# Row sums and shift rows by VectorE's block transposes and transfers instead of by TensorE

## The reference, cut to what matters

```
h = layernorm(x) * (1 + ca) + sa
xq, xk, xv = h @ wq.T, h @ wk.T, h @ wv.T         # 16 heads of 64, 2048 positions each
scores = softmax(xq @ xk.T * 64 ** -0.5)          # per head: 2048 x 2048, fp32
out = scores @ xv
x = x + ga * (out @ wo.T)
```

## Time and profile before

| | |
|---|---|
| median of 3 runs | 1318.63 us (1318.17 to 1810.67) |
| profiled execution, its own time | 1317.36 us |
| its span, first to last instruction | 1315.6 us |
| TensorE busy | 1297.5 us (99%) |
| POOL busy | 1176.0 us (89%) |
| VectorE busy | 911.3 us (69%) |
| ScalarE busy | 888.3 us (68%) |

### The profile page before, as it was taken

One profiled execution on the slowest core, in us unless ns is written; L12 is line 12 of the kernel. 1 busy time (PEld: TensorE's weight loads), 2 busy tenths in 40 slices (PEclk: granted clock), 3 DMA queues, 4 the chain that ended last, 5 costly groups with the idle time before them and its releaser, 6 DMA issues. The chain is left out here.

```text
span 1315.6 us, 22284 instructions
## 1 busy us (share of the span) xinstructions
PE 1297.5 (99%) x8792; PEld 705.3 (54%) x8792; DVE 911.3 (69%) x1036; ACT 888.3 (68%) x1096; POOL 1176.0 (89%) x538
## 2 busy tenths in 40 slices
PE   7999999999999999999999999999999999999998
PEld 5545545454555545454555555454545545454787
DVE  6767667676767677677767676776767676859575
ACT  6666767676766766666766666676767667775474
POOL 2499999999999999999999999999999999999644
PEclk9999999999999999999999999999999999999999
DMA  8010202020110202020100202020200102001323
GB/s 210 11 39 1 49 1 49 1 49 1 27 24 1 49 1 49 1 49 1 38 13 1 49 1 49 2 49 0 49 1 10 40 1 49 1 1 30 101 73 89
DMA packets 31962, 41.55 MB, mean 32 GB/s; under 512 B 4298, under 2 KB 15186, under 8 KB 31858
## 3 DMA queue, kind: packets, MB, share of 16 engines
q1 hardware_dynamic: 31714, 40.13, 12.5%
q10 hardware_dynamic: 144, 0.00, 0.0%
HBM read 13.70 MB, written 1.11 MB: 11 GB/s over the span
## 5 line engine op out<-in xcount | busy, mean ns | idle before, releaser
L918 ACT ACTIVATE probs<-ps 128x1024 f32<-128x1024 f32 x512 | 498.7, 1032 | 78.7 <-PE ps L1348 75.9
L1079 DVE TENSOR_REDUCE peak_parts<-ps 128x2 f32<-128x1024 f32 x297 | 362.2, 1223 | 236.8 <-PE ps L1289 235.1
L1366 PE MATMUL ps<-probs,v_sb 128*64 128x512 f32 x2048 | 522.8, 606 | 0.0
L1009 POOL TENSOR_TENSOR acc<-acc,probs 128x1024 f32<-128x1024 f32 x192 | 457.7, 2384 | 31.2 <-ACT probs L918 29.6
L1009 POOL TENSOR_TENSOR acc_odd<-acc_odd,probs 128x1024 f32<-128x1024 f32 x192 | 459.5, 2393 | 0.0
L860 ACT COPY peak_copy<-ps 128x1024 f32<-128x1024 f32 x215 | 218.6, 1017 | 242.0 <-PE ps L1289 168.0
L1089 DVE TENSOR_REDUCE peak_parts<-peak_copy 128x2 f32<-128x1024 f32 x215 | 260.7, 1212 | 34.2 <-ACT peak_copy L860 34.2
L1366 PEld LDWEIGHTS ps<-probs,v_sb 128*64 128x64 f32 x2048 | 123.8, 136 | 157.3 <-issue 118.4
L1342 PE MATMUL ps<-q_hi,d_swap_hi 64*128 64x512 f32 x512 | 201.4, 393 | 0.4 <-ACT probs L918 0.4
L1342 PE MATMUL ps<-q_hi,d_hi 64*128 64x512 f32 x512 | 201.5, 394 | 0.0
L1348 PE MATMUL ps<-q_hi,d_swap_lo 64*128 64x512 f32 x512 | 200.7, 392 | 0.0
(11 more groups left out here) (237 smaller groups left out, 1571.6 us busy)
## 6 DMA issues: line engine op xcount, KB each, us to landing
k_swap_hi<-k_hi SPq DMA_DIRECT2D x64, 128.0 KB, 2.3
d_swap_hi<-d_hi SPq DMA_DIRECT2D x64, 128.0 KB, 2.3
d_swap_lo<-d_lo SPq DMA_DIRECT2D x64, 128.0 KB, 2.3
q_hi<-weights_dram SPq DMA_DIRECT2D x8, 256.0 KB, 3.2
q_lo<-weights_dram SPq DMA_DIRECT2D x8, 256.0 KB, 4.6
k_hi<-weights_dram SPq DMA_DIRECT2D x8, 256.0 KB, 5.9
k_swap_hi<-weights_dram SPq DMA_DIRECT2D x8, 256.0 KB, 5.3
probs<-in_L_ffn_w_dram SPq DMA_DIRECT2D x2, 512.0 KB, 5.9
```

Source lines behind the costliest of these rows:

```text
L918: act.activation(probs[:, kt % PROBS, :], ps[:, 2 * place:2 * place + 2, :].rearrange("p a b -> p (a b)"), ACT.Exp, scale=SCALE).then_inc( ...
L1009: pool.tensor_tensor(total, total, probs[:, kt % PROBS, :], ALU.add).then_inc(added, 1)
L1079: dve.tensor_reduce(peak_parts[:, :, i // STRETCHES, i % STRETCHES], ps[:, bank:bank + 2, :], AX.X, ALU.max).then_inc(peak_free, 1)
L1366: mm = pe.matmul(ps[at:at + HEAD_DIM, PV_BANK, :], v_sb[:, p, chunk_of(kt) * HEAD_DIM:(chunk_of(kt) + 1) * HEAD_DIM], probs[:, kt % PROBS, ...
```

## The change

- The partition sums of the two accumulators are made by VectorE without a merge: it transposes each accumulator in blocks of 32x32 (even one at place 4, odd one at place 8), reduces each over the 32 elements that came from partitions (places 6 and 10), and folds the four groups of partitions at place 12: a small transpose, five small reductions and a reciprocal of 32x32 elements.
- SP writes the 1024 inverses to DRAM with one DMA, waits for it, and reads them back with two DMAs, each a row of 512 spread over 64 partitions.
- VectorE scales at place 20 (28 in the last unit); both inputs are now in SBUF. The projection moves from place 22 of half 0 to place 14 of half 1, a unit later.
- The maxima are turned by a VectorE transpose of 128x32 behind the peak reduction and sent by eight DMAs instead of two.
- TensorE has no sum matmul and no turn any more, except for the last unit's sum, for which POOL still merges. POOL has 14 adds a unit instead of 15. `acc_odd` gets a second buffer; the even accumulator is transposed into `k_raw`, the odd one into the even accumulator, and the spread row lies in the odd one. ScalarE's copy into `k_raw` waits for the first reduction, POOL's first add of a unit for the scaling of two units before.

```diff
 LONG_JOBS = (
-    {2: ("q", 0), 6: ("sum", 0), 14: ("k", 0), 18: ("k", 1), 22: ("out", 0), 26: ("shift", 0)},
-    {2: ("q", 1), 6: ("v", 0), 10: ("sum", 0), 19: ("v", 1), 26: ("shift", 0)},
+    {2: ("q", 0), 14: ("k", 0), 18: ("k", 1)},
+    {2: ("q", 1), 6: ("v", 0), 14: ("out", 0), 19: ("v", 1)},
 )
+SEND_PLACE = 26
-SCALE_PLACES = (
-    {6: ("inv", 0), 7: ("inv", 1), 8: ("inv", 2), 10: ("inv", 3), 11: ("scale", 0)},
-    {11: ("inv", 0), 12: ("inv", 1), 13: ("inv", 2), 15: ("inv", 3), 16: ("scale", 0)},
-)
+SUM_PLACES = {4: ("turn sum", 0), 6: ("add sum", 0), 8: ("turn sum", 1), 10: ("add sum", 1), 12: ("fold", 0)}
+SCALE_PLACE, LATE_SCALE_PLACE = 20, 28
...
-            def send_shift(job, target_half):
-
-                sp.wait_ge(job_free, job.full)
+            def send_shift(target_unit, target_half):
+
+                sp.wait_ge(peak_turned, target_unit + 1)
                 for odd in (0, 1):
...
+                    for g in range(4):
+                        at = g * 32 + 4 * odd
+                        sp.dma_start(row[:, g], peakT[at:at + 4, target_half, :].bitcast(F32)).then_inc(shift_ready, 16)
+
+            def spread_sums(unit_done):
+
+                parts = SumParts(unit_done)
+                sp.wait_ge(sums_inverted, unit_done + 1)
+                row = sums_dram[unit_done % 2:unit_done % 2 + 1, :]
+                sp.dma_start(row.rearrange("a (j i) -> (a j) i", j=32), parts.inverse).then_inc(sums_out, 16)
+                sp.wait_ge(sums_out, 16 * (unit_done + 1))
+                for b in range(2):
+                    sp.dma_start(parts.spread[b * HEAD_DIM:(b + 1) * HEAD_DIM, :],
+                                 row[:, b * BANK:(b + 1) * BANK].broadcast_to([HEAD_DIM, BANK])).then_inc(sums_spread, 16)
...
+                    dve.wait_ge(peak_ready, target_unit + 1)
...
+                    dve.transpose(peakT[:, target_unit % 2, :].bitcast(F32), peak[:, :].bitcast(F32)).then_inc(peak_turned, 1)
...
+            def turn_sum(unit_done, half_done, odd):
+
+                dve.wait_ge(added, unit_done * ADDS + (ADDS - 1 + odd))
+                dve.transpose(SumParts(unit_done).turned[odd], (acc_odd if odd else acc)[:, half_done, :]).then_inc(sums_turned, 1)
+
+            def add_sum(unit_done, odd):
+
+                parts = SumParts(unit_done)
+                dve.wait_ge(sums_turned, unit_done * 2 + (odd + 1))
+                dve.tensor_reduce(sum_parts[:, odd * 32:odd * 32 + 32],
+                                  parts.turned[odd].rearrange("p (j r) -> p j r", r=32), AX.X,
+                                  ALU.add).then_inc(sums_added, 1)
+
+            def fold_sums(unit_done):
+
+                parts = SumParts(unit_done)
+                dve.wait_ge(sums_added, unit_done * 2 + 2)
+                link(dve.transpose(parts.parts_turned, sum_parts[:, :]))
+                for g in range(4):
+                    ins = dve.tensor_reduce(
+                        parts.quarters[:, g, :],
+                        parts.parts_turned[32 * g:32 * g + 32, :].rearrange("p (a i) -> p i a", a=2), AX.X, ALU.add)
+                link(ins)
+                link(dve.tensor_reduce(parts.sums, parts.quarters.rearrange("p g i -> p i g"), AX.X, ALU.add))
+                dve.reciprocal(parts.inverse, parts.sums).then_inc(sums_inverted, 1)
+
+            def scale_unit(unit_done, half_done):
+
+                dve.wait_ge(sums_spread, 32 * (unit_done + 1))
+                dve.wait_ge(o_copied, unit_done + 1)
+                dve.tensor_tensor(oT[:, half_done, :], o_raw[:, :], SumParts(unit_done).spread,
+                                  ALU.mult).then_inc(out_scaled, 1)
...
+                pe.wait_ge(out_scaled, min(2 * head + 2, UNITS - 1))
```

More of the change, by code:

```diff
@@ L81, in chunk_of, with side_jobs @@
     return half * 8 + pair * 2 + odd
-def side_jobs(half, sums=True, project=True, pairs=True, early=True, last_head=False, before_last=False):
+def side_jobs(half, sums=True, outs=True, project=True, pairs=True, early=True, last_head=False, before_last=False):
     places = [[] for _ in range(4 * PAIRS)]
     for place, (kind, i) in LONG_JOBS[half].items():
-        if sums if kind in ("sum", "out") else pairs if kind == "shift" else project:
+        if outs if kind == "out" else project:
             places[place].append((kind, i))
+    if pairs:
+        places[SEND_PLACE].append(("send", 0))
     if pairs:
@@ L104, in side_jobs @@
     if sums:
-        for place, job in SCALE_PLACES[half].items():
+        for place, job in SUM_PLACES.items():
             places[place].append(job)
+        places[LATE_SCALE_PLACE if last_head and half == 1 else SCALE_PLACE].append(("scale", 0))
     if before_last:
@@ L278, in units @@
                     final_head = last and p == 1
-                    plan = side_jobs(half, sums=not (first and p == 0 and half == 0), project=not final_head,
+                    plan = side_jobs(half, sums=not (first and p == 0 and half == 0), outs=not (first and p == 0),
+                                     project=not final_head,
                                      pairs=not (final_head and half == 1), early=not final_head,
@@ L289, in build @@
             + [("pair", n) for n in range(5, 8)] + PROJECTIONS[4:5] + [("pair", n) for n in range(8, 11)] \
[L290 to L296, removed]
+            + PROJECTIONS[5:] + [("pair", n) for n in range(11, PEAK_PAIRS + EARLY_PAIRS)]
+        PROLOGUE_BANKS = (6, 4, 5, 3, 3, 3)
+        CASTS, SWAPS, D_SWAPS, SENDS = 4, 64, 128, 128
         END_T = HEADS // 2 - 1
@@ L945, in body @@
                         if step == 0 and not first:
-                            copy_pv(unit, sums[-1] if sums else None)
+                            copy_pv(unit)
             pairs_of_heads(body)
-            copy_pv(UNITS, sums[-1])
+            copy_pv(UNITS)
             ffn_act(act)
@@ L1090, in taken @@
                                   ALU.max).then_inc(copy_read, 1)
[L1092 to L1096, removed]
-                dve.tensor_copy(shift_sb[:, target_half, :], job.ps[0:8, 0:P]).then_inc(job_free, 1)
             def invert(part, job):
@@ L1453, in body @@
                                     pair(i, (unit + 2) * PEAK_PAIRS + i, head + 1, 1 - p, half, PEAK_BANK)
-                                if kind == "sum":
-                                    sum_unit(job, unit - 1, 1 - half)
                                 if kind == "out":
@@ L1458, in body @@
                                     heads_out = head
-                                if kind == "shift":
-                                    turn_shift(job, unit + 1)
                                 if kind in ("turn", "logits", "weights"):
```

100 lines of the change are left out of this document (54 added, 46 removed).

## The result

The changed kernel took 1330.5 us (median of 4, 1325.8 to 1331.0) beside 1318.6 of the kernel before (median of 3, 1318.2 to 1319.3): a ratio of 1.008 (95% interval 1.005 to 1.011), no change by the 2% bound. One execution of the kernel before took 1810.7 us; it is a slow run and is left out. The forecast was 1328, the range 1298 to 1362. The profiled execution took 1330.5 us, its span is 1328.6, 13.0 more than before's 1315.6.

The account below looks back on a forecast made before the run. TensorE sets the pace, with VectorE's second beat hidden under it. From the profiled 1317.4 us, +8.4 (full heads) - 0.6 (first head) + 2.0 (prologue) = +9.8 gave 1327, the median 1.3 above: 1328; range 1298 to 1362.

Parts of the forecast that it names:

- Where TensorE's saving goes: Even unit (half 0 of a head): TensorE loses 2.8 us of work, stalls behind VectorE take 2.7; 37.3 against 37.4 us.
- the walk: Place-by-place timing of an even and an odd unit, fitting VectorE's new operations into windows of 1.7 or 2.5 us.
- The odd unit: Half 1 of a head: the projection, now at place 14, covers the fold's delay; 36.06 - 1.07 + 1.75 = 36.75 us.
- The prices: VectorE's new operations: each large transpose 1.15 us, two reductions 2.3, fold 1.7, peak transpose 0.2, scaling 0.9 to 1.5.
- The scaling's phase: Even unit, place 20: scaling issued at 24.7 us, POOL's eighth add ends at 25.0, so the scaling takes 0.9 us.
- The second rival: Even units: the scaling meets a whole POOL addition, 3.0 us instead of 0.9, +31 us, so 1359; chance 0.16.
- The shifts: Eight DMAs for the maxima need 6.9 of 7.3 us and just fit; in the prologue nothing covers them, +2.0 us.
- 14 full heads, +8.4: Full heads between the first and last: each 0.6 us longer, +8.4 us for 14 of them.
- The first head saves 0.6: First head, with no old sums to handle: 0.6 us shorter.
- The last about nothing: Last head: about no change, as the projection moves into its second half and no k work delays VectorE.
- the k swaps: SP's queue: its wait for the inverses stands before these transfers, which are read a unit later; cost nothing.
- first rival: Whole kernel: VectorE's additions hide and TensorE's saving comes through, -33.4 + 2, 1287 us; chance 0.11.

Follow-up runs that it names:

- run 3: Changed kernel with the scaling at place 28 in every unit instead of place 20: 1318.0 us, 0.999 of the kernel before.
- Run 4: Changed kernel with only 32 of 1024 columns of the odd accumulator transposed and reduced: 1310.4 us, 0.994 of the kernel before.
- run 12: Changed kernel with the projection back at place 22 of the next head's first half: 1340.4 us, 1.017 of the kernel before.
- run 8: Changed kernel with POOL merging again, first shifts from two queues, last unit's routing weights ahead of its sums, scaling at place 28: 1406.5 us, 1.066 of kernel before.
- Run 5: Changed kernel with SyncE sending the routing weights' first block before the sums' reciprocals in the last unit: 1325.4 us, 1.0055 of the kernel before.
- run 11: Changed kernel with the edits of run 3 and Run 5 together: 1312.4 us, 0.995 of the kernel before.
- run 10: run 8 with POOL's adds from the eleventh on waiting for the add just ahead: 1305.6 us, 0.991 of the kernel before.
- run 9: run 8 with only the scaling put back from place 28 to place 20: 1322.0 us, 1.003 of the kernel before.

## Why the prediction was right

The median came out 2.5 us above the forecast. The mechanism of the heads was the one forecast; that the number came so near is in part luck. The heads were forecast 5.0 us too long, the two ends 8.2 us too short.

- **Where TensorE's saving goes.** Predicted: 2.8 us less work in an even unit, 2.7 of it eaten by peak pairs behind VectorE, 37.3. Measured in unit 16: pairs late by 0.1 at place 11, 0.5 at 13, 0.4 at 17, 0.1 at 19, 0.8 at 23 and 0.4 at 25, 2.3 in all; 36.9. Places and sizes fit in the main; at 23 the walk had 1.1, at 9 it had 0.1 and none came, and the slip at 25, put down to the scaling, stays when the scaling is moved (run 3). Run 4 shows the cause by itself: with the second transpose and reduction gone the even unit falls to 36.0.
- **The odd unit.** 36.75 predicted, 36.7 measured, and run 12 shows that the projection is the cover it was taken for.
- **The prices.** Transposes 1.15 predicted; 1.235 long and 1.16 from start to the next start (646.23 to 647.39); none of the 62 was stretched by POOL (1.228 to 1.237). Reductions as the copies' reductions. The fold 1.87 (650.86 to 652.73) against 1.7, from four small reductions at 0.21 instead of 0.18. Scaling 0.98 on average, 0.85 in unit 16 against 0.9, half of the 1.9 us that the prediction gave with no regard to where POOL stands.
- **The scaling's phase.** The walk had the scaling issued 24.7 us into the unit and POOL's eighth add ending at 25.0; in unit 16 it was issued at 24.8 and the add ended at 25.1 (rows 662.03, and 659.92 with 2.40 us). It was clear of a whole add by under 0.4 us, a margin that the prediction knew (0.3) and could not be sure of. The second rival's step (a whole POOL add) did not come at place 20, whose scalings took 0.69 to 2.21 us with a median of 0.89, but its price was no fancy: 2.76 us in run 3, 9.9 in run 8. The Trainium skill ("SBUF — State Buffer", section "SBUF: two separate sides") says that of a VectorE operation with two SBUF inputs and POOL's, whichever starts first holds the shared ports for its whole length. Runs 3 and 8 agree that the scaling waits for a whole add; the page says nothing of an operation being passed over three times. The page names only two-port modes and two-input operations as takers; the transposes, which wait for nothing, agree.
- **The shifts.** Predicted to fit in every unit but the first: no other shift matmul shows a wait on its row. VectorE was busy for 29.2 of the 36.9 us of unit 16, 79%, where 84% was predicted.
- **What was mis-sized.** "14 full heads, +8.4" was +3.4 (2.0 in 13 heads, 1.3 in units 28 and 29, where the tail's first layer statistics fall to VectorE too; that these are the cause is not shown): 0.15 us a head instead of 0.6, since the even unit was 0.4 us shorter than walked. "The first head saves 0.6" was +1.7, unit 0 running at the lower clock for its first microseconds. "The last about nothing" was +5.2, and this is the step that failed: it looked at VectorE and TensorE and not at what SyncE's new job stands in front of in that unit. The prediction had asked this of the k swaps in every other unit, not of the routing weights, though their DMA stood in its own rows. Run 5 gives the price: 5 us.
- **What remains of the loss.** With scaling and queue put right (run 11) the same change is 1312.4 us, 0.5% faster than before and 2.5 us faster than its maxima alone; with POOL's merge and pauses for it besides, and the first shifts from two queues (run 10), 1305.6, 0.9% faster. The prediction's first rival (1287) stays out of reach: TensorE still waits for pairs in each version.

## What to carry to other kernels

When work moves from the engine that sets the pace to one that is 70% busy, draw the windows between the moments at which the paced engine needs the other one, and put each added operation into a window in which nobody waits: a 2.8 us operation in an idle window was cheaper here than a 0.85 us one in front of a deadline. Walk the first and the last round for themselves, and there each in-order queue: what does the new job make wait that is due in this round alone? An operation that must share with a saturated engine can need a pause of that engine, and a wait that makes one was worth 96 us here.

## What the runs showed of the hardware

- **VectorE's scaling with both inputs in SBUF can be passed over by POOL several times.** In run 8 eleven scalings took 9.8 to 9.9 us, over three ends of POOL's adds that started 2.29 to 2.35 us apart; where POOL's merge waited for the add ahead, it got in. Where in the add it is issued does not decide by itself: 0.04 us after the start it was passed over (619.24), 0.07 us after the start it was passed over once (1179.25, 9.79 us) and once not (383.86, 2.87 us), and in run 9 it was passed over 0.64 us after; in run 3's even units it entered after one add each time. With the pauses of run 10 none was passed over; they also moved the moment of issue, and what lets POOL keep its place without a pause stays open.
- A block transpose of 128x1024 fp32 in SBUF takes 1.235 us and never waited for POOL; on 32 columns it takes 0.20.
- A 96-element operation with one source (L638) took 2.35 us behind POOL's add in the last unit of the kernel after, as the 12-element one had in the earlier trace rows. The same operation took 0.20 us in the kernel before (1194.54), where it began 0.02 us ahead of POOL's add: short operations pay the wait as fully as long ones, and only when they come second.
